# Attention over four heads at a time: values in two goes of eight matmuls, a ring of five turned heads, and the spread of the inverse moved to GpSimd

## The reference, cut to what matters

```python
# x (8, 512, 512), 16 heads of D=32, mask (512, 512) bool, cond (8, 128)
q, k, v = proj(Wq), proj(Wk), proj(Wv)                 # (8, 16, 512, 32)
scores = einsum('bhsd,bhtd->bhst', q, k) * D**-0.5
attn = softmax(where(mask, -inf, scores), axis=-1)     # 8*16 matrices of 512x512
out = einsum('bhst,bhtd->bhsd', attn, v) ... @ Wo.T
y = rmsnorm(out) * rms_scale * (1 + sc) + shift        # sc, shift from silu(cond) @ Wc.T + bc
x = x + y
x = x + rotate(x)     # per token and column d a 4x4 matrix over the four quarters of the row
```

## Time and profile before

| | us |
|---|---|
| median of 3 runs | 988.27 (987.57 to 989.47) |
| span of the profiled execution, first to last instruction | 986.2 |
| own time of the profiled execution | not given; the median is 2.1 above the span |
| PE busy in the span | 912.2 |
| DVE, ACT, POOL busy | 707.5, 638.8, 523.6 |

### The profile page before, as it was taken

One profiled execution on the slowest core, in us unless ns is written; L12 is line 12 of the kernel. 1 busy time (PEld: TensorE's weight loads), 2 busy tenths in 40 slices (PEclk: granted clock), 3 DMA queues, 4 the chain that ended last, 5 costly groups with the idle time before them and its releaser, 6 DMA issues.

```text
span 986.2 us, 20466 instructions
## 1 busy us (share of the span) xinstructions
PE 912.2 (92%) x6278; PEld 648.2 (66%) x6278; DVE 707.5 (72%) x1581; ACT 638.8 (65%) x1523; POOL 523.6 (53%) x441
## 2 busy tenths in 40 slices
PE   7999999999968989999999998999999999999980
PEld 5788888888845557666666665666666666666650
DVE  4522132223168888989999898899999899898878
ACT  5222222223158888888888887788888888888820
POOL 0999930000001122677666776566677666776665
PEclk9999999999979999999999999999999999999995
DMA  8855465544878547756666745666665576455111
GB/s 282 303 188 193 170 223 189 183 171 181 186 249 185 118 98 181 164 117 151 150 140 139 194 108 129 152 155 145 142 161 125 133 187 156 109 120 139 33 54 43
DMA packets 82325, 153.98 MB, mean 156 GB/s; under 512 B 8472, under 2 KB 9112, under 8 KB 82224
## 3 DMA queue, kind: packets, MB, share of 16 engines
q1 hardware_dynamic: 82224, 152.75, 57.6%
HBM read 102.35 MB, written 50.36 MB: 155 GB/s over the span
## 4 chain that ended last, share of the span: by engine, by line
PE 59%; issue 6%; DVE 5%; POOL 1%; DVEq 0%; ACT 0%; POOLq 0%
PE prob_ps L663 27%; PE out_ps L679 15%; PE score_ps L647 12%; DVE probs_T L770 2%; PE y_ps L700 2%; PE y_ps L701 1%; PE y_ps L702 1%; PE out_ps L689 1%; DVE probs L528 1%; POOL probs L1008 1%; DVE probs L754 0%; DVE probs L824 0%; DVE probs L836 0%; DVEq L520 0%; DVE probs L831 0%
## 5 line engine op out<-in xcount | busy, mean ns | idle before, releaser
L867 ACT ACTIVATE probs<-probs,least 128x512 f32<-128x512 f32 x512 | 364.3, 716 | 32.0 <-DVE inv_den L763 25.4
L663 PE MATMUL prob_ps<-ident,probs 128*128 128x128 f32 x2048 | 314.5, 281 | 26.2 <-DVE probs_T L770 25.4
L754 DVE CUSTOM_DVE_ANT_0 probs<-score_ps,mask_bias 128x512 f32<-128x512 f32 x512 | 333.1, 679 | 4.4 <-PE score_ps L647 4.4
L663 PEld LDWEIGHTS prob_ps<-ident,probs 128*128 128x128 f32 x2048 | 227.4, 141 | 159.2 <-issue 117.7
L647 PE MATMUL score_ps<-k_rows,q_rows 128*128 128x512 f32 x512 | 240.4, 477 | 12.5 <-PEq L78 9.3
L770 DVE COPY probs_T<-prob_ps 128x512 f32<-128x512 f32 x256 | 175.4, 685 | 65.0 <-PE prob_ps L663 63.1
L874 ACT ACTIVATE probs_T<-prob_ps 128x512 f32<-128x512 f32 x256 | 153.2, 598 | 76.7 <-PE prob_ps L663 72.6
L271 DVE SCALAR_TENSOR_TENSOR late<-proj,late 128x512 fp32r<-128x512 f32 x64 | 44.0, 690 | 181.3 <-ACT late L240 181.2
L679 PE MATMUL out_ps<-probs_T,v_sb 128*32 128x256 f32 x2048 | 163.0, 391 | 0.0
L528 POOL TENSOR_TENSOR late<-rot,late 128x2048 f32<-128x2048 f32 x26 | 119.1, 4580 | 66.8 <-DVE late L787 66.8
L940 POOL TENSOR_TENSOR o_T<-raw_T 128x256 f32<-128x256 f32 x64 | 47.9, 748 | 142.3 <-ACT raw_T L882 142.3
(11 more groups left out here) (112 smaller groups left out, 1349.1 us busy)
## 6 DMA issues: line engine op xcount, KB each, us to landing
q_rows<-q_scratch SPq DMA_DIRECT2D x128, 256.0 KB, 5.8
k_rows<-k_scratch SPq DMA_DIRECT2D x128, 256.0 KB, 6.7
q_scratch<-late SPq DMA_DIRECT2D x64, 256.0 KB, 2.3
k_scratch<-late SPq DMA_DIRECT2D x64, 256.0 KB, 2.3
v_scratch<-v_out SPq DMA_DIRECT2D x32, 256.0 KB, 2.0
v_sb<-v_scratch SPq DMA_DIRECT2D x8, 1024.0 KB, 10.9
raw<-in_xT SPq DMA_DIRECT2D x7, 1024.0 KB, 5.6
late<-in_x SPq DMA_DIRECT2D x28, 256.0 KB, 2.7
```

The costliest lines, as they stand in the source:

```text
L663: last = pe.transpose(prob_ps[:, r % 2, j * HALF + c * P:j * HALF + (c + 1) * P], probs[:, s % 2, r // 2 * 2 + c, key:key + P], ident[:, :])
L754: dve.tensor_tensor_reduce(probs[:, s % 2, r, :], score_ps[:, r % 4, :], mask_bias[:, c, :], 1.0, 3e38, ALU.add, ALU.min, least[:, s % 2, ...
L867: act.activation(probs[:, s % 2, r, :], probs[:, s % 2, r, :], ACT.Exp, bias=least[:, s % 2, r:r + 1], scale=-1.0, accum_out=den[:, s % 2, ...
```

## The change

Units are no longer halved: a turned head is kept whole (512 queries) in a ring of five head slots, `probs` is a ring of 12 tiles, and all orders are written out for the 512 tiles with no loop. Removed lines are those of the functions above; the new ones, cut:

```diff
+RING, SLOTS = 12, HG + 1
+SCORE_AHEAD, MASK_AHEAD, EXP_AHEAD = 10, 6, 4
+VALUES_AT, SCALE_AT, PROJECT_AT = (1, 3), 3, 4
+NORM_AT, INVERT_AT, RESCALE_AT, RESIDUAL_AT, SQUARE_AT = 5, 0, 1, 3, 0
+BURST, SKIPS = 2, (7, 12)
...
-        probs_T = sb("probs_T", [P, 2, HG, TC, HALF])
+        turned_probs = sb("turned_probs", [P, SLOTS, TC, S])
...
 # PE
+            def turn(n):
+                pe.wait_ge(exped, n + 1)
+                place_free(pe, place(n) - 2)
...
-                for i in range(HG):
-                    last = pe.matmul(value_ps[i * D:(i + 1) * D, :], v_sb[:, p, j, h * D:(h + 1) * D],
-                                     probs_T[:, s % 2, i, j, :], ...)          # 256 columns, one j a call
+                for j in (2 * part, 2 * part + 1):
+                    for i in range(HG):
+                        last = pe.matmul(value_ps[i * D:(i + 1) * D, :], v_sb[:, b % 2, j, h * D:(h + 1) * D],
+                                         turned_probs[:, (HG * u + i) % SLOTS, j, :], ...)   # 512 columns
...
+            for n in range(N):
+                u, t = n // TILES, n % TILES
+                if t in VALUES_AT and u > 0:
+                    values(u - 1, VALUES_AT.index(t))
+                if t == SCALE_AT and u > 0:
+                    turn_scale(u - 1)              # waits for spread; takes a place in turn_ps
+                if n + SCORE_AHEAD < N:
+                    score(n + SCORE_AHEAD)         # waits for masked, n + 7
+                if u >= NG and 0 <= t - PROJECT_AT < 12:
+                    project(u - NG, t - PROJECT_AT, y_ps[:, :])    # one matmul of the twelve
+                turn(n)
...
 # DVE
-                dve.tensor_copy(inv_den[:, :, :, :], inv_sum[:, :, :].unsqueeze(3).to_broadcast([P, 2, HG, D]))
+                dve.reciprocal(inv[:, :, :], den[:, u % 2]).then_inc(inverted, 1)
+            def norm(u):                           # waits for valued, scale_out, o_ready
+                dve.tensor_tensor(o_T[:, :], value_ps[:, :], inv_T[:, :], ALU.mult).then_inc(normed, 1)
...
+                if t == INVERT_AT and u > 0:
+                    invert(u - 1)
+                for _ in range(BURST if t in VALUES_AT else 0 if t in SKIPS else 1):
+                    mask(done); done += 1
+                if t == RESCALE_AT and u > NG: rescale(u - NG - 1)
+                if t == RESIDUAL_AT and u > NG: residual(u - NG - 1)
+                if t == NORM_AT and u > 0: norm(u - 1)
+                if not by_act(n - 1) and n > 0: move_out(n - 1)
...
 # ACT: exp as mask, four ahead; then
+                if t == SQUARE_AT and u > NG: square(u - NG - 1)
+                if t == SCALE_AT and u > 0: move_scale(u - 1)      # turn_ps to inv_T, 128x512
+                if by_act(n - 1) and n > 0: move_out(n - 1)
...
 # POOL
+            def spread_inverse(u):
+                pool.tensor_copy(inv_d[:, :, :, :], inv[:, :, :].rearrange("p i c -> p c i").unsqueeze(3)
+                                 .to_broadcast([P, TC, HG, D])).then_inc(spread, 1)
...
+            for u in range(U):
+                spread_inverse(u - 1); rms(u - NG - 1); split(u - 1); rotate(u - NG - 1); shift(u - NG)
```

More of the change, by code:

```diff
@@ L530, in rotation_products @@
                                      ALU.mult)
[L532 to L552, removed]
+        tail_scaled = [turned_probs[:, 0, c, :] for c in range(TC)]
+        tail_mix = probs[:, 0:TC, :]
+        tail_out = [probs[:, TC + c, :] for c in range(TC)]
+        tail_x = [v_sb[:, 0, c, :] for c in range(TC)]
         tail_in = [sem(f"tail_in{c}") for c in range(TC)]
@@ L635, in _ @@
         def _(pe):
[L636 to L664, removed]
-                last.then_inc(turned, 1)
@@ new lines, in turn, with turn_scale @@
+            def turn(n):
+                pe.wait_ge(exped, n + 1)
+                place_free(pe, place(n) - 2)
+                for j in range(TC):
+                    last = pe.transpose(turn_ps[:, place(n) % 2, j * P:(j + 1) * P], probs[:, n % RING, j * P:(j + 1) * P],
+                                        ident[:, :])
+                last.then_inc(turned, 1)
+            def turn_scale(u):
+                pe.wait_ge(spread, u + 1)
+                place_free(pe, scale_place(u) - 2)
+                for c in range(TC):
+                    last = pe.transpose(turn_ps[:, scale_place(u) % 2, c * P:(c + 1) * P],
+                                        inv_d[:, c].rearrange("p i d -> p (i d)"), ident[:, :])
+                last.then_inc(scale_turned, 1)
@@ L699, in project @@
+            def project(m, part, y):
+                b, c = m // TC, m % TC
+                k, way = part // 3, part % 3
+                if way == 0:
+                    pe.wait_ge(o_ready, NG * b + k + 1)
+                if part == 0 and 0 < m < CHUNKS:
+                    pe.wait_ge(scaled_ready, m)
                 t = slice(c * P, (c + 1) * P)
-                pe.matmul(y[:, :], o_hi[:, p, k, t], wo_hi[:, k, :], start=(k == 0), stop=False)
-                pe.matmul(y[:, :], o_hi[:, p, k, t], wo_lo[:, k, :], start=False, stop=False)
@@ L726, in _ @@
-            for r in range(TILES + SCORE_AHEAD):
-                score(0, r // TILES, r % TILES)
-            batch(0, 0, first=True)
-            batch(1, 1)
-            with pe.Fori(2, B - 3, 2) as b:
-                batch(b, 0)
-                batch(b + 1, 1)
-            batch(B - 2, 0)
-            batch(B - 1, 1, last=True)
-            for k in (2, 3):
-                project(B - 2, 0, TC - 1, k, y_ps)
-            for j in range(TC):
-                value(B - 1, STEPS - 1, 1, j)
-            turn_scale(STEPS * B - 1)
@@ L745, in _ @@
+            for part in range(2):
+                values(U - 1, part)
+            turn_scale(U - 1)
+            for parts in (range(9), range(9, 12)):
+                for c in range(TC):
+                    for part in parts:
+                        project(CHUNKS + c, part, score_ps[:, c, :])
         @block.vector
         def _(dve):
-            def mask(b, s, r):
-                n = STEPS * b + s
-                dve.wait_ge(scores, TILES * n + r + 1)
-                if not known(n, 2):
-                    dve.wait_ge(turned, TILES * (n - 2) + r // 2 * 2 + 2)
-                take_waits(dve)
-                c = 2 * (s % 2) + r % 2
-                dve.tensor_tensor_reduce(probs[:, s % 2, r, :], score_ps[:, r % 4, :], mask_bias[:, c, :], 1.0, 3e38,
-                                         ALU.add, ALU.min, least[:, s % 2, r:r + 1]).then_inc(masked, 1)
@@ L807, in _ @@
-            for r in range(TILES + MASK_AHEAD):
-                mask(0, r // TILES, r % TILES)
-            batch(0, 0, first=True)
-            batch(1, 1)
-            with dve.Fori(2, B - 3, 2) as b:
-                batch(b, 0)
-                batch(b + 1, 1)
-            batch(B - 2, 0)
-            batch(B - 1, 1, last=True)
-            rescale(B - 2, 0, TC - 1)
+            done = 0
+            for n in range(MASK_AHEAD):
+                mask(n)
+            done = MASK_AHEAD
+            for n in range(N):
+                u, t = n // TILES, n % TILES
+                if t == INVERT_AT and u > 0:
+                    invert(u - 1)
+                for _ in range(BURST if t in VALUES_AT else 0 if t in SKIPS else 1):
+                    if done < N:
+                        mask(done)
+                    done += 1
+                if t == RESCALE_AT and u > NG:
+                    rescale(u - NG - 1)
+                if t == RESIDUAL_AT and u > NG:
+                    residual(u - NG - 1)
+                if t == NORM_AT and u > 0:
+                    norm(u - 1)
+                if not by_act(n - 1) and n > 0:
+                    move_out(n - 1)
```

510 lines of the change are left out of this document (227 added, 283 removed).

## The result

The changed kernel takes 990.59 us (median of 20 runs, 987.88 to 996.52), the kernel before 988.47 (20 runs, 986.25 to 989.79): ratio 1.0028, 95% interval 1.0014 to 1.0041. It is slower by 0.28%, where 949 was forecast, in a range of 922 to 975. The profiled run is one of the longer ones, 995.83 with a span of 994.0, so what is read in its trace comes out larger than in the median.

What follows compares the result with a forecast made beforehand. PE was taken as the bound, with one small wait a unit. A unit of 18.66 work plus 0.95 waits is 19.6 us, 1.2 less; 28 units save 34, first units 3, head 1.6: 39 together, 949 us, range 922 to 975.

Steps and rivals of the forecast that it cites:

- the last of the new waits: SP's queue: store and load of x behind load_unit have more than 5 us before the shift; wait hidden.
- Rival 4: Slower: the round over POOL, norm back to norm, sets the pace if the spread is dear; 1002 us, chance 0.11.
- The spread: Spread of 512 elements on POOL, taken as two casts: 0.8 us, at most 4.6.
- The prediction's own sign of being wrong: Wrong if the chain names POOL or a wait behind the goes; other signs were unit lengths near 20.1 or 18.8.
- PE's values: Two goes of 1.93 us a unit, 3.86 in place of 5.12: 1.26 us less; change-over 0.21 us a call.
- PE's work in all: PE's work a unit without waits: 19.72 + 0.2 − 1.26 = 18.66 us.
- The masks: Unit's first score waits 0.7 us on PE for DVE's mask, the mask of the tile before 0.2.
- The copy ahead of the first go: First go waits for ACT's copy of the last tile; hidden by the first score's wait, otherwise 0.6 us.
- DVE and the spread: DVE loses two spreads of 1.16 us a unit and gains norm, 0.69: from 19.1 to 17.5.
- The first units: Four first units, without projection, 19.1 us each before: 0.8 us less each, 3 in all.
- The head: Seven masks in place of ten ahead of the first turn, ready at 288.0 not 289.6: 1.6 us less.
- Rival 2: No new waits: a unit is 18.66 + 0.2, saving 2.0 × 28 + 5 = 61 us; 927 us, chance 0.12.

Runs made afterwards that it cites:

- x_first: Changed kernel with the load of x issued at the start of a unit's transfers, not behind row loads, v or mod, and store; 961.15 us, ratio 0.9719.
- x_same_time: Changed kernel with x issued at the same event, but ahead of the unit's row loads and v or mod; 961.14 us, ratio 0.9720.
- goes_of_256: skip_at_0 with each value matmul of 512 columns made as two of 256, in the same goes; 922.68 us.
- square_at_1: skip_at_0 with ScalarE's square and VectorE's rescale each one tile later; 917.20 us, ratio 0.9278.
- skip_at_0: x_first with masks and exponentials left out at tiles 0 and 7, not 7 and 12, and begun one tile further ahead; 921.63 us, ratio 0.9324.
- spread_on_dve: skip_at_0 with the spread of the inverse as one copy behind the reciprocal on DVE, GpSimd's gone; 922.19 us.

## Why the prediction was wrong

- **The step that failed** is the last of the new waits: "SP: behind `load_unit`, which waits for scores, stand the store and the load of x; they have more than 5 us before the `shift` that needs them. Hidden." The time that was left was right: in the unit shown x is issued 5.8 us before POOL is ready for the shift (543.95 to 549.76). What is missing is a term for the landing. At the head of the queue, as in the kernel before, that is 2.7 us in the median; behind the rows, and in some units behind mod or v, it is 9.3 in the median and up to 12.2. Put at 0, the wait costs 21.08 − 19.84 = 1.24 us a unit in the profiled run, of which at most 9.2 / 26 = 0.35 are matmuls slowed by the clock, and 29.4 us between the medians, as x_first and x_same_time show by taking it away alone. A row of the page before gave a sign that this transfer was tight, since the shift waited for it even then:

```profile
L953 POOL TENSOR_TENSOR late<-late,mod_b 128x512 f32<-128x512 f32 x28 | 36.0, 1284 | 39.7 <-DMA late<-in_x 39.7
```

- **POOL's round.** Rival 4 had POOL on the path (norm to norm over POOL), for the wrong reason: with x early POOL is idle 6.8 us a unit, and a second spread costs nothing. What holds POOL is a transfer that starts when the scores of the unit are made. The spread was sized a little high, 0.61 against 0.8. The prediction's own sign of being wrong, a chain that names POOL, came: POOL is 4% of the chain that ended last where it was 1%.
- **PE's values.** Right in mechanism and size: 1.86 a go against 1.93, so 2 × 1.86 = 3.72 a unit in place of 5.12, and 13.9 us for two more calls a unit against 13 expected. The gain is in the 16 changes made 4, since the width of 512 columns brings nothing by itself: sets of 512 cost twice those of 256 (goes_of_256). TensorEngine Tiling of the Trainium skill (Key Properties) says that a change of tiling mode drains TensorE. The 0.24 us for a further call agrees with it; that a drain is what the time goes into, no run here shows.
- **PE's work in all** was set 0.3 too high, 18.66 against 18.34 in square_at_1. Of this 0.14 is the goes (3.86 against 3.72); where the rest lies was not looked into.
- **The masks.** The place was right (the unit's first score, and one just before); 0.9 was forecast, the waits read 0.48 + 0.59, and skip_at_0 gave 1.32 a unit, more than the two waits. That turns and copies behind them had been late too is likely, but not shown. The copy ahead of the first go: "hidden by the first wait. If the first were gone, this would cost 0.6" was right in kind: it appeared in skip_at_0 at 0.2, and square_at_1 took 4.4 us from the total (0.16 a unit).
- **DVE and the spread.** Off the path once x is early and the masks have their slack: with the spread back on DVE the time is the same. In the kernel before, what cost was its standing, 1.77 us of the copy for 256 elements in front of PE's and ACT's waits; it is mostly gone when the copy meets a short operation of GpSimd. So with these orders one copy a unit on DVE does as well as the move to GpSimd; with the change's own orders it was not tried. SBUF — State Buffer of the Trainium skill (Who interferes with whom) describes a lock between such copies and GpSimd for a whole instruction. The trace agrees: the copy ends 0.15 to 0.28 us after GpSimd's operation. `norm`, which by the same rule takes no part, took 0.68 to 0.69 us in every unit.
- **The first units** were to gain 0.8 each. The 19.1 for the kernel before mixes two marks (first turn and first shift). From value call to the same call two units on it is (356.66 − 317.93) / 2 = 19.37, and (363.56 − 325.44) / 2 = 19.06 in the change, so 0.3 was gained. They too lived by the masks, since skip_at_0 brings them to 18.15. **The head** gained nothing in the profiled run (first turn at 289.7) and 1.7 in x_first (287.95), which has the same head. **The tail** is 44.4 us from the end of the last turn, 1.3 more.
- Rival 2, "no new waits", gave 927: that is where the kernel comes, at 922 and 917, once x is early and the masks have their slack.

So the place of a transfer and the place of the masks' slack took back all that the change gained. Put right, the kernel is 71 us under the one before. Read by unit, 20.83 has become 18.34: 1.40 less for the goes, about 0.9 for the wait that PE had for DVE, 0.13 for the loop. Of the 73.4 us between the change and the fastest version, x's place is 29.4, the masks' slack 39.5 and the square's place 4.4, in this order; the middle one shows only when the first is cured.

## What to carry to other kernels

A transfer that feeds a chain of work belongs ahead of large transfers that are only needed a unit later; price its landing behind what is queued in front of it, not by its landing in the kernel before. When an order is rewritten, list for each queue what has moved ahead of what, and follow each moved item to its waiter. When one repair brings nothing, a longer wait may run beside it: try the repairs together.

## What the runs showed of the hardware that was not expected

The same 256 KB load of x takes 2.8 us (median, x_same_time) to land ahead of the others and 9.3, up to 12.2, behind 2 to 3 MB of other loads from the same queue; issuing it takes 0.35 us ahead and 0.43 behind. Value matmuls in 32-column strips cost the same per column with 256 and 512 columns. Where the spread on DVE meets a GpSimd operation it ends 0.15 to 0.28 us after that operation, in the kernel before and in spread_on_dve. In the unit shown two waits of PE, 1.66 and 1.56 us, were followed by about 3 us at half the granted clock, so that a wait on another engine's transfer made matmuls slower as well.

The runs of the change scatter over 9 us and those of x_first over 1. The ten shorter runs of the change have a mean granted clock of 0.976 and the ten longer ones of 0.974; that x's landing varies, and the clock with it, is the likely cause, but it is only argued.
